# The last superblock of the second attention takes its two query blocks one after the other, two key tiles a slot

## The reference, cut to what matters

```python
x = x + conv_attn(group_norm(x))       # first attention: softmax(q k^T) v with projections, times gamma, and a gated x
t = to_tokens(x)
n = layernorm(t)
t = t + softmax(n n^T) n               # second attention, no projections
u = layernorm(t)
probs = softmax(u @ router_w + router_b)           # 8 experts
top_p, top_i = top_k(probs, 2); top_p = top_p / sum(top_p)
t = t + sum over the two of top_p * (u @ expert_w[top_i] + expert_b[top_i])
```

## Time and profile before

| what | us |
|---|---|
| three runs: lowest, median, highest | 2653.24, 2655.68, 2656.77 |
| the profiled execution's own time | 2656.39 |
| its span in the profile | 2654.7 |
| PE busy | 2580.9 (97%) |
| DVE busy, ACT busy | 2111.8 (80%), 1945.9 (73%) |
| POOL busy | 453.8 (17%) |

### The profile page before, as it was taken

How to read it: one execution, slowest core, us unless ns; L and a number is a source line. 1 busy time by engine, 2 the same in 40 slices (tenths; PEclk the granted TensorE clock), 3 DMA queues, 4 the chain that set the end, 5 groups by cost and what they waited for, 6 DMA issues and landing times.

```text
span 2654.7 us, 46190 instructions
## 1 busy us (share of the span) xinstructions
PE 2580.9 (97%) x15334; PEld 2374.7 (89%) x15334; DVE 2111.8 (80%) x6216; ACT 1945.9 (73%) x3732; POOL 453.8 (17%) x840
## 2 busy tenths in 40 slices
PE   7999999999999999999999999999999999999996
PEld 5889998899988998889988899888998899988995
DVE  6886788878888688886788877888778876887675
ACT  4767876778677786777866778677786778767784
POOL 0000221012210131101311014010240002300124
PEclk9999999999999999999999999999999999999998
DMA  1000000000000000000000000000000000000000
GB/s 38 1 19 1 4 10 1 22 4 7 7 1 22 4 7 7 22 1 4 10 4 22 1 4 10 4 22 1 4 10 4 22 1 4 13 1 4 1 10 13
DMA packets 11323, 23.17 MB, mean 9 GB/s; under 512 B 1360, under 2 KB 7760, under 8 KB 11088
## 3 DMA queue, kind: packets, MB, share of 16 engines
q1 hardware_dynamic: 11088, 20.20, 2.2%
HBM read 10.76 MB, written 9.44 MB: 8 GB/s over the span
## 4 chain that ended last, share of the span: by engine, by line
PE 79%; DVE 8%; ACT 8%; issue 4%; POOL 1%; DMA 0%; ACTq 0%; SPq 0%; POOLq 0%; DVEq 0%
PE ps L1103 22%; PE ps L1105 22%; PE ps L1104 22%; PE ps L1116 12%; ACT row_space L681 3%; DVE row_space L913 2%; DVE pt_lo L928 2%; ACT row_space L727 1%; ACT pt_hi L692 1%; DVE tn_tok L979 1%; ACT xg_hi L636 1%; DVE pt_lo L1002 0%; ACT pt_hi L736 0%; PE ps L1261 0%; DVE gn_raw L800 0%
## 5 line engine op out<-in xcount | busy, mean ns | idle before, releaser
L692 ACT ACTIVATE pt_hi<-ps 128x384 fp32r<-128x384 f32 x864 | 420.9, 489 | 305.7 <-PE ps L1116 303.3
L928 DVE TENSOR_TENSOR pt_lo<-ps,pt_hi 128x384 fp32r<-128x384 f32 x864 | 473.5, 553 | 153.3 <-ACT pt_hi L692 147.0
L1002 DVE TENSOR_TENSOR pt_lo<-row_space,pt_hi 128x768 fp32r<-128x768 f32 x432 | 419.2, 972 | 149.1 <-ACT pt_hi L736 148.5
L727 ACT ACTIVATE row_space<-ps,shift 128x768 f32<-128x768 f32 x432 | 390.2, 903 | 167.6 <-PE ps L1105 164.4
L913 DVE TENSOR_SCALAR_CACHE_REDUCE row_space<-ps 128x512 f32<-128x512 f32 (+1 forms) x720 | 450.8, 631 | 55.6 <-PE ps L1105 49.3
L1116 PE MATMUL ps<-ident,row_space 128*128 128x128 f32 x2736 | 447.4, 273 | 14.0 <-ACT row_space L681 12.7
L681 ACT ACTIVATE row_space<-row_space,negmax 128x512 f32<-128x512 f32 (+2 forms) x432 | 403.6, 934 | 63.7 <-DVE negmax L922 63.7
L1116 PEld LDWEIGHTS ps<-ident,row_space 128*128 128x128 f32 x2736 | 343.0, 140 | 97.7 <-ACT row_space L681 25.8
L736 ACT ACTIVATE pt_hi<-row_space 128x768 fp32r<-128x768 f32 x432 | 366.3, 848 | 40.7 <-PE ps L1105 1.1
L1103 PE MATMUL ps<-pt_hi,v_hi 128*128 128x384 f32 x864 | 357.4, 414 | 8.5 <-ACT y_out L701 7.7
L1103 PE MATMUL ps<-xt_hi 128*128 128x384 f32 x864 | 302.5, 350 | 0.0
(11 more groups left out here) (174 smaller groups left out, 5133.4 us busy)
## 6 DMA issues: line engine op xcount, KB each, us to landing
x_chan<-x SPq DMA_DIRECT2D x24, 384.0 KB, 3.9
y<-y_out SPq DMA_DIRECT2D x48, 192.0 KB, 1.9
t_tok<-eb SPq DMA_DIRECT2D x1, 516.0 KB, 5.6
t_tok<-ew SPq DMA_DIRECT2D x1, 516.0 KB, 6.5
row_space<-wqkv SPq DMA_DIRECT2D x1, 192.0 KB, 3.3
se_sb<-se SPq DMA_DIRECT2D x1, 68.0 KB, 4.7
biases<-channel SPq DMA_DIRECT2D x1, 2.0 KB, 4.9
```

Of the source, the lines that this page charges most:

```text
L692: act.activation(pt_hi[:, slot, :], ring_bank(step)[:, 0:BW], ACT.Copy)\
L727: act.activation(p1_f[:, w % 2, :].rearrange("p (s w) -> p s w", s=2), ps[:, 2 * (w % 2):2 * (w % 2) + 2, 0:BW], ACT.Exp, bias=shift[:, :])\
L928: dve.tensor_tensor(pt_lo[:, slot, :], ring_bank(step)[:, 0:BW], pt_hi[:, slot, :], ALU.subtract).then_inc(pt_lo_ready, 1)
L1002: dve.tensor_tensor(p1_lo[:, w % 3, :], p1_f[:, w % 2, :], p1_hi[:, w % 3, :], ALU.subtract).then_inc(p1_lo_ready, 1)
```

## The change

In superblock 2 of every batch, slots 36 to 44 now belong to query block 4 and slots 45 to 53 to query block 5; each slot takes two key tiles for one block in place of one key tile for two. The matmuls are as many and as wide as before. Bank 4 is complete after `pv1` 44, in slot 46, and bank 5 after `pv1` 53, in slot 55; each is copied out alone by a new step `o1half`. Bank 4 joins the turn of side banks in slot 46.

In batches 0 to 6 `o1t`/`o1add` of block 4 move from slot 57 to slot 50 and those of block 5 from 59 to 57. Batch 7 gets tables of its own: `LAST_O1_SLOTS` and `LAST_MOE_SLOTS`, by which block 4's expert stage ends in slot 56 and only block 5's stands after the attention.

```diff
 O1_SLOTS = [20, 29, 38, 40]
+
+LAST_O1_SLOTS = [20, 23, 38, 40, 47, 56]
+LAST_MOE_SLOTS = [(5, 9, 11, range(13, 19), 20), (21, 23, 25, range(26, 32), 33), (28, 32, 33, range(34, 40), 40),
+                  (39, 41, 42, [43, 43, 44, 44, 45, 45], 46), (42, 46, 47, [48, 48, 49, 49, 50, 50], 51),
+                  (48, 51, 52, [53, 53, 54, 54, 55, 55], 56), (57, 59, 60, range(61, 67), 68)]
...
+def one_block(b, w):
+
+
+    return w >= (LB - 1) * NT
...
-    for m, slot in enumerate(O1_SLOTS):
+    for m, slot in enumerate(LAST_O1_SLOTS if b + 1 == B else O1_SLOTS):
         merge(beside, {slot: [("o1t", b, m), ("o1add", b, m)]})
     blocks = [(b - 1, 5)] + [(b, m) for m in range(4)]
-    for (c, m), slots in zip(blocks, MOE_SLOTS):
+    for (c, m), slots in zip(blocks + [(b, 4), (b, 5)], LAST_MOE_SLOTS if b + 1 == B else MOE_SLOTS):
         if c >= 0:
             merge(beside, moe(c, m, *slots))
     if b + 1 < B:
         merge(beside, early(b + 1))
     if b + 1 < B:
         merge(beside, {end + j: attention0(b + 1, 1, j) for j in range(NT)})
-        merge(beside, {end + 3: [("o1t", b, 4), ("o1add", b, 4)], end + 5: [("o1t", b, 5), ("o1add", b, 5)]})
-    else:
-        merge(beside, {end + 2: [("o1t", b, 4), ("o1add", b, 4)], end + 3: [("o1t", b, 5), ("o1add", b, 5)]})
-        merge(beside, moe(b, 4, end + 3, end + 5, end + 6, range(end + 8, end + 14), end + 15))
-        merge(beside, moe(b, 5, end + 11, end + 13, end + 14, range(end + 16, end + 22), end + 23))
+        merge(beside, {50: [("o1t", b, 4), ("o1add", b, 4)], end + 3: [("o1t", b, 5), ("o1add", b, 5)]})
...
             s.append(("pv1", b, w - LAG))
-            if (w - LAG) % NT == NT - 1:
+            if one_block(b, w - LAG):
+                if (w - LAG) % (NT // 2) == NT // 2 - 1:
+                    s.append(("o1half", b, (w - LAG) // (NT // 2) - 2 * (LB - 1)))
+            elif (w - LAG) % NT == NT - 1:
                 s.append(("o1evac", b, (w - LAG) // NT))
         if not opens:
             s += first
...
         given = {("s1", LB * NT - 1): ((0, 1), ("s1", b, LB * NT - 2)), ("pv1", LB * NT - 2): ((2, 3), ("s1", b, LB * NT - 1)),
-                 ("o1evac", LB - 1): ((4,), step)}.get((kind, step[-1]))
+                 ("o1evac", LB - 1): ((4,), step), ("o1half", 0): ((4,), step)}.get((kind, step[-1]))
...
+                elif kind == "o1half":
+                    h = step[2]
+                    act.wait_ge(pv1_done, at(pv1_done, "pv1", b, (LB - 1) * NT + (h + 1) * (NT // 2) - 1))
+                    act.wait_ge(ring_full, filled(("o1t", b, h)))
+                    act.activation(o1_chan[0][:, h * BW:(h + 1) * BW], ps[:, 4 + h, 0:BW], ACT.Copy).then_inc(o1_chan_ready, 1)
...
                         elif b:
-                            pe.wait_ge(o1_chan_ready, at(o1_chan_ready, "o1evac", b - 1, LB - 1))
+                            pe.wait_ge(o1_chan_ready, at(o1_chan_ready, "o1half", b - 1, 1))
...
                     tile = slice(j * 128, (j + 1) * 128)
                     for i in range(2):
                         cols = slice(ib * LW + i * BW, ib * LW + (i + 1) * BW)
+                        if one_block(b, w):
+                            h, t = divmod(2 * j + i, NT)
+                            tile = slice(t * 128, (t + 1) * 128)
+                            cols = slice(ib * LW + h * BW, ib * LW + (h + 1) * BW)
                         ins = three(ps[:, 2 * (w % 2) + i, 0:BW], xt_hi[:, tile], xt_lo[:, tile], xt_hi[:, cols],
                                     xt_lo[:, cols])
...
                     for i in range(2):
                         cols = slice(i * BW, (i + 1) * BW)
-                        ins = three(ps[:, 4 + i, 0:BW], tn_hi[:, j, :], tn_lo[:, j, :],
-                                    p1_hi[:, w % 3, cols], p1_lo[:, w % 3, cols], start=j == 0, stop=j == NT - 1)
+                        h, t = divmod(2 * j + i, NT) if one_block(b, w) else (i, j)
+                        ins = three(ps[:, 4 + h, 0:BW], tn_hi[:, t, :], tn_lo[:, t, :],
+                                    p1_hi[:, w % 3, cols], p1_lo[:, w % 3, cols], start=t == 0, stop=t == NT - 1)
                     ins.then_inc(pv1_done, 1)
                 elif kind == "o1t":
                     m = step[2]
-                    pe.wait_ge(o1_chan_ready, at(o1_chan_ready, "o1evac", b, m // 2))
+                    if m >= 4:
+                        pe.wait_ge(o1_chan_ready, at(o1_chan_ready, "o1half", b, m - 4))
+                    else:
+                        pe.wait_ge(o1_chan_ready, at(o1_chan_ready, "o1evac", b, m // 2))
```

More of the change, by code:

```diff
@@ L240 @@
     "s1": ["s1_done", "p1_exp_ready", "p1_hi_ready"], "p1low": ["p1_lo_ready"], "pv1": ["pv1_done"], "o1evac": ["o1_chan_ready"],
+    "o1half": ["o1_chan_ready"],
     "o1t": ["ring_full"], "o1add": ["o1_added"], "uln": ["u_var_ready", "u_rstd_ready"], "uapply": ["u_tok_ready"],
@@ L245 @@
 }
-LAST = {"score": "score_ready", "s1": "p1_exp_ready", "o1evac": "o1_chan_ready", "fold": "bias_left", "gn_dev": "gn_dev_ready", "gn_var": "gn_var_ready", "se_in": "se_hidden_ready", "se_out": "se_exp_ready",
+LAST = {"score": "score_ready", "s1": "p1_exp_ready", "o1evac": "o1_chan_ready", "o1half": "o1_chan_ready", "fold": "bias_left", "gn_dev": "gn_dev_ready", "gn_var": "gn_var_ready", "se_in": "se_hidden_ready", "se_out": "se_exp_ready",
         "kproj": "k_lo_ready", "vproj": "v_lo_ready", "baset": "base_tok_ready",
```

## The result

The changed kernel takes 2661.46 us (median of 11 runs, 2657.21 to 2664.0), the kernel before in the same job 2655.96 (11 runs, 2653.24 to 2656.77): a ratio of 1.0021, 95% interval 1.0012 to 1.0030. It is slower by 5.5 us. The prediction was 2654.0 with a range of 2645 to 2658, so the time lies outside it, on the side that was given 9 in 100. The profiled execution ran 2661.93.

The account below looks back on a forecast made before the run. PE's work was taken to bound all but the end, an engine-to-engine chain the end. Batch 7 without waits ends at 2641.7; waits of 11.3 make 2653.0, less 1.7 than 2654.7, so median 2654.0, range 2645 to 2658.

Parts of the forecast that it names:

- the price of a wait: Batch 7's last attention: each wait of PE that the new table makes counted at its own length, 11.3 us in sum.
- What bounds the kernel, the end behind the attention: PE's work bounds all but the end, an engine-to-engine chain the end; there a chain of 17 us goes.
- 24.1 + 1.4: Behind batch 7's attention: one block's chain of 24.1 us, plus 1.4 for block 5's power waiting behind block 4's tiles on POOL.
- Two tiles a slot, `o1half`: Second attention, all batches: as many, wide and long matmuls, no shared weight loads lost, ACT has room for the copies: 0.
- Batches 0 to 6: Moved `o1add` in slot 50 covered by 1 us: 0; gain at most 4 in all, loss at most 13.
- Rival B: Slot 50 of batches 0 to 6: DVE's 1.9 us not covered, PE waits seven times, 13.3 us, 2667; chance 0.10.
- Block 1's `yt`: Batch 7, slot 40: PE waits 2.1 us for POOL's third tile, that tile taken at 3.0 us.
- Block 2's bank: Batch 7: the second `expert` needs tile 0's bank, which DVE frees at 6.9 while PE comes at 5.6: wait 1.4 us.
- Block 2's `yt`: Batch 7: POOL ends the third tile at 16.1 us from slot 43's start, PE comes at 13.9: wait 2.1 us.
- Block 3: Batch 7, from slot 47: 0.8 us lost for banks, then a wait at `yt` for POOL's tile; 4.3 us in all.
- rival A: Batch 7's attention: ACT, DVE and POOL catch up while PE stands, waits only 3 to 6 us, middle 2648.5; chance 0.33.

Follow-up runs that it names:

- experiment 2: Changed kernel, but batch 7 keeps the old expert slots, with only block 4's `o1t` and `o1add` moved to slot 50: 2656.8 us, ratio 1.0005.
- experiment 8: Changed kernel with `yt` of blocks 1 to 4 one slot later, and `o1t`/`o1add` of batches 0 to 6 back in their old slots: 2651.11 us, ratio 0.9981.
- experiment 4: Changed kernel with 12 idle matmuls of 384 columns ahead of PE's `yt` wait in blocks 1 to 3 of batch 7: 2659.47 us, ratio 1.0014.
- Experiment 3: Changed kernel with every `yt` of blocks 1 to 4 in batch 7 one slot later, nothing else: 2652.56 us, ratio 0.9987.
- experiment 5: Changed kernel with only DVE's order in batch 7 altered (statistics of blocks 3 and 4, block 4's `o1add`, each one slot later): 2661.7 us, ratio 1.002.
- experiment 1: Changed kernel with the change in batch 7 alone, batches 0 to 6 as in the kernel before: 2657.98 us, ratio 1.0011.
- experiment 6: Changed kernel with `yt` of blocks 1 to 4 one slot later, DVE's order altered, and block 0's `ut` in slot 24: 2652.02 us, ratio 0.9984.
- experiment 7: Changed kernel with batch 7's table one slot looser and batches 0 to 6 as in the kernel before: 2647.09 us, ratio 0.9967.

## Why the prediction was wrong

The step that failed is the price of a wait: the sum put each wait of PE at its own length and nothing for the clock behind it, which took 5.1 us (three times 3.4 us at half the clock). Two terms put at 0 were smaller: batches 0 to 6 (2.2 us over the seven) and block 0's `ut` (1.3). Term by term:

- **What bounds the kernel, the end behind the attention**: right, in size too. From the last exponential to the end 13.4 us went. From PE's last attention work (the `o1t` at 2634.65 starts right behind block 4's last expert matmuls) to the end it is 25.5 us, against the 24.1 + 1.4 of the sum. The 1.4 was for block 5's power, which waits for block 4's tile on POOL (2638.99 and 2639.55 above).
- **Two tiles a slot, `o1half`: 0.** Right: experiments 2 and 8.
- **Batches 0 to 6: 0.** Wrong: 2.2 us, 0.3 a batch. The bounds of -4 to +13 held it. What failed is that I looked only at slots 49 to 51. There the cover holds: PE's waits for the second attention's low parts are 6.1 us in sum over batches 0 to 6, where they were 5.8. The price comes later, in the next batch's first attention, where PE's transposes wait for ACT's exponentials. Rival B named the step that costs, but not the place (low parts and banks at slot 50) nor the size, 1.9 a batch.
- **The waits, one by one.** Block 1's `yt` 2.1: measured 2576.29 - 2574.18 = 2.1. Its third tile on POOL 3.0: 2573.25 to 2576.24. Block 2's bank 1.4: 1.2 idle. Block 2's `yt` 2.1: 2.2. Block 3 4.3 (0.8 for banks and 3.5 at `yt`): 3.15 idle at `yt`, 3.3 with the handing over, and none for banks. POOL was through with its third tile 20.7 us after slot 47 began (2621.17 - 2600.45), where I had 19.8: I gave that tile 2.26 as undisturbed, and it took 3.7, as the rows below show. The wait on PE was no longer for it only because PE came 17.6 us after slot 47 began (2621.23 - 3.15 - 2600.45) and not 16.8: it lost no 0.8 for banks, but 1.7 by the slower clock in slot 47. One wait I had not at all: 1.08 at block 0's `ut`, in slot 23. Without it PE stood 8.4 us in the attention, against 9.9 in the sum: the working of the waits was right in kind and nearly in size. That with the 1.08 it is 9.5 is two misses that offset each other.

  Block 3's third tile on POOL, and what DVE did meanwhile:

```profile
2617.51 0.46 POOL L614 TENSOR_TENSOR row_space<-row_space 128x128 f32<-128x128 f32 x1
2617.93 1.17 POOL L615 TENSOR_TENSOR row_space<-row_space 128x128 f32<-128x128 f32 x1
2619.07 1.17 POOL L617 TENSOR_TENSOR acc<-acc,row_space 128x128 f32<-128x128 f32 x1
...
2620.72 0.45 POOL L621 TENSOR_TENSOR acc<-acc,row_space 128x128 f32<-128x128 f32 x1
```

```profile
2617.64 1.15 DVE L1018 TENSOR_TENSOR pt_lo<-row_space,pt_hi 128x768 fp32r<-128x768 f32 x1
2618.95 0.97 DVE L1018 TENSOR_TENSOR pt_lo<-row_space,pt_hi 128x768 fp32r<-128x768 f32 x1 [0.16 <-ACT pt_hi L747]
```

  Each of the two long additions ends 0.3 us behind a low part of DVE (2619.10 behind 2618.79, 2620.24 behind 2619.92). I had taken POOL as undisturbed because PE stands by then; but DVE still has the low parts of the slots before to make. The Trainium skill, SBUF — State Buffer, section "SBUF: two separate sides", has the two engines lock each other out of a shared port pair for just these kinds of operation; the trace agrees, and the place to apply it was here too.
- **The term that was missing: the clock behind a wait.** I priced each wait at its own length. Rows of the profile of before showed the other price, 0.72 as the mean clock where PE stands much, but only behind the attention, and I did not ask what waits of 2 to 3 us would do in the midst of it. They cost 1.7 us each on top, 5 in all, and experiment 4 shows that it is the clock: with as long a wait but PE kept at work, 3.6 of them are back in the profiled attention.

From the predicted 2653.0 to the measured span of 2660.2: clock +5.1, batches 0 to 6 with the start +0.8 (batch 7 begins at 2470.0, not 2469.2), `ut` of block 0 with its handing over +1.3, the waits of blocks 1 and 2, so counted, +0.3 (5.9 against 5.6), block 3 -1.0, the end 0. Sum 6.5 of 7.2; 0.7 are not traced. Less the 5.1 of the clock the median would be 2656.4, inside the range, and so the clock decided it. The chances followed from that: rival A, which got a third, needed the other engines to catch up while PE stands; three waits of about the forecast size say that they don't. Experiment 3 says why: a third tile takes from PE's matmuls to `acc` about two slots, and `yt` had been given one. It was a matter of a slot, not of the order of DVE's work (experiment 5).

## What to carry to other kernels

When a written order makes the busiest engine wait, count the slots between the producer's first step and its consumer against the whole latency of the chain between them (here 4.4 us from the third pair's end at 2571.84 to `acc` at 2576.24, against a slot of 2.1), and move the consumer by one slot before rebalancing any engine. Price a wait of the tensor engine within a dense stretch at its length, and then look for the clock behind it: here 1.7 us for each of the three waits of 1.86 to 3.15 us. A step moved earlier to help the last of eight repetitions can be paid for in the other seven (0.3 us each here): make it conditional on the last.

## What the runs showed of the hardware

- A wait of PE of 1.85 to 3.3 us within an otherwise full stretch can bring the clock to its lower level (granted clock 0.50), matmuls of 384 columns starting 0.32 us apart and not 0.17. Five times that held for 3.4 us and began 0.2 to 1.2 us behind the wait's end; twice, at the waits of 3.13 (experiment 1) and 3.30 (experiment 5), it held for 6.8 us and began about 1 us before the wait ended. Not each wait does it: of nine such waits in three kernels (the changed one, experiments 1 and 5) seven did; one of 1.85 (experiment 1) and one of 2.72 (experiment 5) did not:

```profile
2600.28 0.55 PE L1132 MATMUL ps<-ident,acc 128*128 128x128 f32 x3 [2.72 <-POOL acc L621]
...
2600.00:2610.00 10.00, 9.72 (x58) 9.21 (x59) 6.01 (x20) 6.18 (x12) 0.52 (x2) 1.00 0.06 21
```

  Of the waits of 1.03 to 1.67 us within an attention (17, over the changed kernel and experiments 1 and 3 to 8) none did. Nor did the three filled waits of experiment 4. What decides in between stays open. It fits that the changed kernel's two runs at 2657.2 had a mean granted clock of 0.997 and the others, up to 2664.0, 0.994 or 0.995. But the kernel before, with no such wait in its attention, has the same link: 2653.06 us at 0.996, 2657.95 at 0.993. So not all of the scatter is those waits.
- The start of the program, up to the first exponential of batch 0, took from 199.1 to 202.9 us in profiled executions, with no relation to the edits. A difference of 3 us between two single executions can be that alone, and is better read between marks within the program.
